# Embedding interaction tower: half of the bilinear units with the batch on the partitions, their sums over 64 on the free axis

## What is computed

```python
def _L0_rec_ref(emb_inputs, kernel):
    ...
    p = emb_inputs[:, ROW_IDX]
    q = emb_inputs[:, COL_IDX]
    return jnp.einsum('bne,hne,bnh->bn', p, kernel, q)
...
z = _L0_rec_ref(e, L0_rec_kernel)
h = jnp.concatenate([z, dense_ctx], axis=1)
h = jnp.maximum(h @ W_top1 + b_top1, 0.0)
h = jnp.maximum(h @ W_top2 + b_top2, 0.0)
y = h @ W_top3
```

## Time and profile before

| what | value |
|---|---|
| median of 3 runs | 486.28 us (486.17 to 489.33) |
| the profiled execution, its own time | 487.89 us |
| its span (first to last instruction) | 486.1 us |
| granted TensorE clock over the span | 0.995 of full |

### The profile page before, as it was taken

The page is one execution under the profiler, slowest core; times in us unless marked ns, Lnnn a source line. Parts: engine busy times, 40 slices in busy tenths (PEclk is TensorE's granted clock), DMA queues, the critical chain, the costliest instruction groups (busy, mean ns, idle before and its releaser), DMA issues.

```text
span 486.1 us, 8241 instructions
## 1 busy us (share of the span) xinstructions
PE 429.2 (88%) x3552; PEld 273.3 (56%) x3552; DVE 306.3 (63%) x321; ACT 35.3 (7%) x69; POOL 242.0 (50%) x260
## 2 busy tenths in 40 slices
PE   0225999999999999999999999999999999999976
PEld 0114665555566765555566766555566766555545
DVE  0114687777777367777776367777776367777730
ACT  1000000000011100000011100000011100000002
POOL 5777777777777777736077776506074000000000
PEclk9999899999999999999999999999999999999999
DMA  5787851111111111101011111001011000000000
GB/s 126 165 173 172 197 159 28 27 27 28 27 27 28 28 26 29 29 16 24 2 26 28 28 27 29 18 6 23 2 26 21 1 2 1 1 0 1 1 1 0
DMA packets 13620, 19.20 MB, mean 39 GB/s; under 512 B 5584, under 2 KB 6928, under 8 KB 13584
## 3 DMA queue, kind: packets, MB, share of 16 engines
q1 hardware_dynamic: 5392, 10.27, 9.1%
q0 software_dynamic: 8192, 8.40, 8.8%
HBM read 18.65 MB, written 0.00 MB: 38 GB/s over the span
## 4 chain that ended last, share of the span: by engine, by line
PE 69%; issue 12%; DVE 9%; POOL 6%; DMA 2%; ACT 1%; DVEq 0%
PE bil L390 35%; PE z_ps L412 24%; DVE prod L333 8%; POOL gathered L252 6%; PE side_ps L426 5%; PE side_ps L432 2%; PE bil L426 1%; DMA gathered<-in_tbl,ids_sb 1%; PE bil L359 1%; PE bil L432 1%; PE side_ps L438 1%; DMA ids_sb<-in_ids 0%; ACT emb L272 0%; DVE inner L329 0%; DVE inner L327 0%
## 5 line engine op out<-in xcount | busy, mean ns | idle before, releaser
L333 DVE TENSOR_TENSOR prod<-bil,emb 128x1024 f32<-128x1024 f32 x224 | 259.8, 1216 | 129.6 <-PE bil L390 127.6
L252 POOL DMA_INDIRECT gathered<-in_tbl,ids_sb x256 | 241.8, 944 | 129.3 <-issue 75.6
L390 PE MATMUL bil<-emb,k_sb 64*128 64x256 f32 x2048 | 257.4, 395 | 15.2 <-DVE prod L333 10.3
L390 PEld LDWEIGHTS bil<-emb,k_sb 64*128 64x128 f32 x2048 | 191.8, 191 | 79.3 <-DVE prod L333 32.7
L412 PE MATMUL z_ps<-prod,sel_sb 128*32 128x512 f32 x960 | 116.5, 595 | 2.3 <-DVE prod L333 2.3
L412 PEld LDWEIGHTS z_ps<-prod,sel_sb 128*32 128x32 f32 x960 | 30.0, 110 | 70.8 <-issue 59.7
L359 PE MATMUL bil<-ident_sb,gathered 64*128 64x64 f32 x256 | 15.2, 241 | 34.7 <-DMA gathered<-in_tbl,ids_sb 34.3
L272 ACT ACTIVATE emb<-bil 128x512 f32<-128x512 f32 x32 | 19.1, 596 | 287.7 <-PE bil L359 287.7
L325 DVE TENSOR_TENSOR prod<-bil,emb 128x512 f32<-128x512 f32 x32 | 21.8, 682 | 27.9 <-PE bil L390 27.9
L359 PEld LDWEIGHTS bil<-ident_sb,gathered 64*128 64x128 f32 x256 | 12.6, 147 | 44.8 <-issue 26.4
L412 PE MATMUL z_ps<-inner,sel_sb 128*32 128x512 f32 x64 | 29.1, 602 | 0.0
(11 more groups left out here) (17 smaller groups left out, 23.1 us busy)
## 6 DMA issues: line engine op xcount, KB each, us to landing
k_sb<-in_k_blocks SPq DMA_DIRECT2D x24, 256.0 KB, 5.1
gathered<-in_tbl,ids_sb POOLq DMA_INDIRECT x256, 2.5
k_sb<-in_k_blocks SPq DMA_DIRECT2D x8, 192.0 KB, 6.3
inner<-in_dense_rows SPq DMA_DIRECT2D x64, 1.0 KB
w_sb<-in_w SPq DMA_DIRECT2D x1, 1024.0 KB
k_sb<-in_k_blocks SPq DMA_DIRECT2D x8, 64.0 KB, 4.9
w_sb<-in_w SPq DMA_DIRECT2D x1, 512.0 KB
ids_sb<-in_ids SPq DMA_DIRECT2D x1, 128.0 KB, 2.2
```

The lines of the kernel that those rows point to most:

```text
L252: pool.indirect_dma_start(gathered[:, n % GATHER_RING, t, f * EMBED:(f + 1) * EMBED], None, tables[field], bass.IndirectOffsetOnAxis(ap=id ...
L333: dve.tensor_tensor(out, x_y[:, :, :], both.to_broadcast([P, 2, BANK]), ALU.mult)\
L390: last = pe.matmul(out[:, s, i * w:(i + 1) * w], k_sb[rows, n, :], e[rows, j, :], start=True, stop=True)
```

## The change

Of the 64 units of a chunk, 32 stay as they were (8 inner units and 24 "fields" units). The other 32 become "batch" units: the same work on 16 pairs of fields by 128 samples in place of 8 pairs by 256.

- `bilinear`: the weights are now the samples (`emb`, 64x128) and the moving operand four matrices side by side (`k_sb`, 64x512): two matmuls in place of four, the same columns in all. Samples come out on the partitions, 16 pairs x 64 numbers on the free axis.
- DVE multiplies 128x1024 by the gathered rows themselves (not the transposed ones) into a new ring `rows_prod` of four units (`ROWS_RING`).
- The sum over 64 is now on the free axis. For three of four batch units ACT makes it: 16 activations (copy) of 128x64 with an accumulator output, each writing its row back in place and one number into `z_rows`. For the fourth (`v % 4 == 3`) DVE makes it with one `tensor_reduce` of 128x1024.
- `reduce_batch` on PE is left only for the other 32 units, after every four of them (`BATCH_UNITS` = 4, `REDUCE_LAG` = 3 units later), into one bank for the whole chunk; `prod` has 6 slots.
- The dense layers get a fifth piece ahead, "turn": four 128x128 transposes of `z_rows`, which wait for all sums of the chunk, and one more copy on ACT in place of the second `copy_z`. The pieces now stand at units 6, 18, 25, 34 and 41 of the next chunk.
- All 32 fields of a chunk's gathered rows stay in SBUF for two chunks; from the third chunk on, POOL gathers when the chunk two before is multiplied. Quads are transposed four units ahead of their use, not three.

```diff
@@ -9,54 +9,112 @@
...
+BATCH_PAIRS = [0, 0, 2, 2, 2, 3, 3, 4]
 
 
 def unit_list():
-
-
     units = []
     for k in range(QUADS):
...
+        while batch or fields:
+            if len(batch) >= len(fields):
+                units.append(batch.pop(0))
+            else:
+                units.append(fields.pop(0))
     return units
...
+VECTOR_SUMS = {v for v in range(NB) if v % 4 == 3}
+NV, NA = len(VECTOR_SUMS), NB - len(VECTOR_SUMS)
+
+BIL_RING, PROD_RING, ROWS_RING, IN_RING = 3, 6, 4, 4
+BATCH_UNITS = 4
+BATCHES = NS // BATCH_UNITS
+REDUCE_LAG = 3
+SUM_LAG = 2
...
@@ -244,99 +312,145 @@
             pool.wait_ge(ids_loaded, 16)
             for n in range(NQUAD):
                 q, k = divmod(n, QUADS)
-                if n >= GATHER_RING:
-                    pool.wait_ge(quad_transposed, n - GATHER_RING + 1)
+                if q >= 2 and k == 0:
+                    pool.wait_ge(unit_multiplied, (q - 1) * NU)
...
+            def sum_rows(u):
+                q, (_, part, t) = u // NU, UNITS[u % NU]
+                v = batched_before(u)
+                if v % NB in VECTOR_SUMS:
+                    return
+                act.wait_ge(unit_multiplied, u + 1)
+                if q >= 2 and v % NB == 0:
+                    act.wait_ge(head_done, (q - 2) * len(PIECES) + 1)
+                col = 16 * FIRST_PARTS.index(part)
+                for x in range(16):
+                    row = rows_prod[:, v % ROWS_RING, x, :]
+                    last = act.activation(row, row, ACT.Copy, accum_out=z_rows[:, q % 2, t, col + x:col + x + 1])
+                last.then_inc(scalar_summed, 1)
...
+                if PIECES[i] == "turn":
+                    act.activation(z_sb[:, 2:4, :].rearrange("p g b -> p (g b)"), bank[:, 0:BANK], ACT.Copy).then_inc(head_kept, 1)
...
             for u in range(NUNIT):
                 for n in TRANSPOSED_AT[u]:
                     keep_quad(n)
+                if u >= SUM_LAG and UNITS[(u - SUM_LAG) % NU][0] == "batch":
+                    sum_rows(u - SUM_LAG)
...
+                if kind == "batch":
+                    v = batched_before(u)
+                    if v >= ROWS_RING:
+                        free_rows(v - ROWS_RING)
+                    row = gathered[:, q % 2, t, 2 * c * EMBED:(2 * c + 8) * EMBED].unsqueeze(1)
+                    dve.tensor_tensor(rows_prod[:, v % ROWS_RING, :, :].rearrange("p (j x) h -> p j (x h)", j=2),
+                                      x_y[:, :, :], row.to_broadcast([P, 2, BANK]), ALU.mult).then_inc(unit_multiplied, 1)
+                    return
...
+                dve.tensor_reduce(z_rows[:, q % 2, t, col:col + 16], rows_prod[:, v % ROWS_RING, :, :], AXIS.X, ALU.add)\
+                   .then_inc(vector_summed, 1)
...
+                if kind == "batch":
                     for s in range(2):
                         rows = slice(s * EMBED, (s + 1) * EMBED)
-                        if m is not None:
+                        last = pe.matmul(out[:, s, :], e[rows, m, t * P:(t + 1) * P],
+                                         k_sb[rows, 2 * part:2 * part + 4, :].rearrange("p n h -> p (n h)"),
+                                         start=True, stop=True)
+                    last.then_inc(unit_done, 1)
+                    return
...
+                if PIECES[i] == "turn":
+                    pe.wait_ge(scalar_summed, (q + 1) * NA)
+                    pe.wait_ge(vector_summed, (q + 1) * NV)
...
```

More of the change, by code:

```diff
@@ L15 @@
 HIDDEN1, HIDDEN2 = 512, 256
[L16 to L19, removed]
+CHUNK = 256
+CHUNKS = BATCH // CHUNK
+CT = CHUNK // P
 TILES = BATCH // P
@@ L25, with part_list @@
 BANK = 512
+GROUPS = 4
+def part_list():
+    parts = []
+    for k in range(QUADS):
+        parts.append((k, None, None))
+        for m in (2 * k, 2 * k + 1):
+            parts += [(k, m, 2 * cp) for cp in range(k)]
+    return parts
+PARTS = part_list()
+NPART = len(PARTS)
+BATCH_PAIRS = [0, 0, 2, 2, 2, 3, 3, 4]
 def unit_list():
@@ L32, in unit_list @@
     for k in range(QUADS):
-        units.append((k, None, None))
-        for m in (2 * k, 2 * k + 1):
-            units += [(k, m, 2 * cp) for cp in range(k)]
+        own = [n for n in range(NPART) if PARTS[n][0] == k]
+        units.append(("inner", own[0], 0))
+        couples = [(x, m) for x in range(0, k - 1, 2) for m in range(2)][:BATCH_PAIRS[k]]
+        firsts = [own[1 + m * k + x] for x, m in couples]
+        batch = [("batch", n, t) for n in firsts for t in range(CT)]
+        fields = [("fields", n, 0) for n in own[1:] if n not in firsts and n - 1 not in firsts]
+        while batch or fields:
[3 more added lines that the diff above has]
+                units.append(fields.pop(0))
     return units
@@ L76, in slot_row @@
 def slot_row(slot):
-    s = slot % 64
-    return slot // 64, 32 * (s % 4) + 2 * (s // 4)
+    return 32 * (slot % 4) + 2 * (slot // 4)
 def z_row(b, side):
[L83 to L87, removed]
+    s, n = divmod(b, 2 * NPART)
+    part, i = divmod(n, 2)
+    for first in (part, part - 1):
+        if first in FIRST_PARTS:
+            at = 16 * FIRST_PARTS.index(first) + 8 * s + 4 * (part - first) + 2 * i + side
+            return 2 + at // P, at % P
+    u = [v for v in range(NU) if UNITS[v][:2] in (("inner", part), ("fields", part))][0]
+    a = summed_before(u)
+    if UNITS[u][0] == "fields":
+        return i, slot_row(2 * a + s) + side
     if i == 1 and side != s:
[L89 to L93, removed]
+        return 0, slot_row(2 * a + 1) + side
+    return (s, slot_row(2 * a) + side) if i == 0 else (0, slot_row(2 * a) + s)
 FREE_ROWS = sorted({(g, r) for g in range(GROUPS) for r in range(P)}
@@ L101, in dense_of @@
 def dense_of(k, side):
-    bank, row = slot_row(2 * FIRST_OF[k] + 1)
-    return FREE_ROWS.index((2 * bank + 1, row + side))
+    return FREE_ROWS.index((1, slot_row(2 * summed_before(FIRST_OF[k]) + 1) + side))
 def pair_index(i, j):
@@ L185, in interaction_tower, with inner_batch @@
         block = ctx.enter_context(nc.Block())
[L187 to L193, removed]
+        def inner_batch(n):
             q, k = divmod(n, QUADS)
-            return q * NU + FIRST_OF[k]
+            return summed_before(q * NU + FIRST_OF[k]) // BATCH_UNITS
         @block.sync
@@ L261, in keep_quad @@
                 act.wait_ge(quad_transposed, n + 1)
-                if q >= 2:
+                if q >= 2 and k == 0:
                     act.wait_ge(unit_multiplied, (q - 1) * NU)
[L264 to L271, removed]
@@ L301, in _ @@
                     keep_head(*HEAD_AT[u], side_ps)
[L302 to L306, removed]
+            for u in range(NUNIT - SUM_LAG, NUNIT):
+                if UNITS[u % NU][0] == "batch":
+                    sum_rows(u)
+            keep_head(CHUNKS - 1, 0, side_ps)
+            copy_z(CHUNKS - 1)
+            for i in range(1, len(PIECES)):
                 keep_head(CHUNKS - 1, i, bil[i % BIL_RING][:, 0, :])
```

267 lines of the change are left out of this document (153 added, 114 removed).

## The result

The changed kernel takes 543.45 us (median of 4 runs, 542.18 to 543.92) against 487.8 for the kernel before (four runs, three of them those given ahead): a ratio of 1.1125, 95% interval 1.1052 to 1.1199. It is 11% slower. Its profiled execution took 542.18 us with a span of 540.4.

The account below looks back on a forecast made before the run. ScalarE was to bound the kernel at 101.8 us a chunk: first sum at 51, sums 378, other work 24, edges 48, end 19, around the span 1.8: 522 us profiled, 520 median; 8 in 10 range 450 to 640.

Parts of the forecast that it names:

- signs given: Middle chunks: ACT busy over 85%, DVE's idle time before L405 released by ACT, PE some 70%, a chunk near 118 us.
- What the change takes from PE and gives DVE: Per chunk: PE's reductions 14.3 us in place of 28.6, PE's sum 84.2; DVE gains 8 `tensor_reduce` of 1.1, sum 84.0.
- Rival (d): On PE, the 64x512 matmul takes 1.72 us, adding 27.5 us a chunk, 112 in all; about 520 us; chance 0.03.
- The step of ScalarE: One small activation with its accumulator readout on ACT takes 246 ns, the middle of 196 and 296; ends 124 and 396.
- that case: On ACT, activation and accumulator readout overlap at both ends: 124 + 72 = 196 ns a step.
- Rival (a): ACT's sums are cheap, 124 ns a step, holding up to about 180; PE and DVE bound; 456 us; chance 0.27.
- ScalarE becomes the bound: ACT's sum is 101.8 us a chunk, 18 more than PE's or DVE's.
- The failed step: A quad's copy on ACT stands behind up to three sums, 11.8 us; PE's wait for it was given nothing extra.
- The sum, term by term: Whole kernel: first sum at 51, 96 sums 378, ACT's other work 24, three edges 48; last sum ends at 501.
- The turn: At each chunk's edge ACT waits about 5 us for PE to make the transposes of `z_rows`.
- Handing over: In the kernel before, a chunk's 11 us over PE's sum of 98 are the handing over between PE and DVE.
- Rival (b): Three engines equally full at 196 ns a step, 22 us handing over, chunk 106, kernel about 480 us; chance 0.13.

## Why the prediction was right, and where it was off

The forecast was 522 us for the profiled execution and 520 for the median; measured 542.2 and 543.4. The direction held, and ScalarE's sums are what costs, but the size was short by 4%, and ScalarE's pace reaches PE by another way than forecast. Of the signs given, DVE's idle time before L405 was to be released by ACT: 14.1 us are, 71.9 by PE. PE's busy share fell to 78%, not 70, and a chunk takes 122.8, not 118.

*What the change takes from PE and gives DVE.* Right. `tensor_reduce` is 1206 ns long (1.1 taken for its pace), the products with the gathered rows 1215, the 64x512 matmuls run side by side: a unit takes 1.13 us beside DVE, as now. Rival (d) falls. DVE's sum was 84.0 and is 85.7 busy.

*The step of ScalarE.* 246 ns forecast, 239 measured, but by a way other than argued, and so by some luck. I had an activation of 224 ns, a readout of 172, and an overlap lost between them. They are 243 and 189 ns, and both boundaries overlap by 0.1 us: 145 + 94. By my own lengths that case was 196. The 243 ns agrees with the page of the Trainium skill that was weighed, "VectorE: DVE Perf Modes", section "The TRN2 errata — SBUF-src ops pay a fixed extra latency per instruction": by it an estimated 240 ns were to be expected for 64 elements from SBUF, and here the rows of PSUM sources misled by 19 ns. That page's difference between the two sources, an estimated 43 ns from its 52 cycles, is larger than these 19. The run without accumulator agrees with the other page of the Trainium skill, "ScalarE: Activation LUTs", section "What ACT_TABLE_LOAD costs": an estimated 146 ns a step by the page, 0.146 us measured. The PSUM rows agree with its lengths less well than the prediction says: 172 ns for two elements, where it gives an estimated 188. Rival (a)'s condition was false, but its time was right to 3%: with a step of 0.146 us the kernel takes 468, with next to none 463, against 456.

*ScalarE becomes the bound.* It is the fullest engine whose time is not stretched by the clock: 100.0 us a chunk, forecast 101.8. The run without accumulator shows that the sums' length is a cause: 75 us come and go with 93 ns a step. But "bound" was too strong. With the same sums on ScalarE and the copies elsewhere the kernel takes 497, so its busy share of 81% in a chunk (I wrote over 85%) was the sign of something else.

*The failed step* is the sentence "PE waits there too, but only while ACT is behind anyway, so I add nothing for it". The quads' copies behind sums are no free wait. They stop PE three times a chunk, the clock is at its lower level behind each of these waits, and DVE has nothing to multiply (it stands idle 5.22 us behind PE's wait of 5.29). ScalarE is idle 22.8 us in a chunk where I had 16 (5.4 for the piece `l2` of the dense layers, which stands behind PE's wait of 5.29, 4.8 for the turn, 4.1 for transposed quads, 2.8 for `copy_z`, the rest in small waits), and the run with the copies on DVE puts the price of their place at 9 us of idle time a chunk and their own work at 4. The sum, term by term: first sum at 52.3 (51); 96 sums 367 (378); other work 27 (24); idle time until the last sum, which ends at 519.1, 73 (48); from there to the end of the span 21.3 (19.0). The idle time is 25 us over, and the cheaper step hides 11 of them: that the total is only 20 us off is in part luck. At the end PE had waited 9.04 us for the last sums, and the last reduction took 3.59 us at the lower clock, where I had 1.8:

```profile
519.11 1.08 PE L535 MATMUL side_ps<-ident_sb,z_rows 128*128 128x128 f32 x4 [9.04 <-ACT rows_prod L349]
520.12 3.59 PE L524 MATMUL z_ps<-prod,sel_sb 128*32 128x512 f32 x16
```

*How much of that is the clock* stays open. PE's busy time in a chunk is 104.1 with the copies on ScalarE, 99.5 with them on DVE and 96.6 with almost no sums, so the stretches at half clock add some 5 to 8 us of busy time; no run kept the waits and took the clock away. Two things bound it. The sums placed later gave 25 us with the clock unchanged (0.907), so those came from the waits. And from the clock over the span (0.908 of 540 us) PE spent an estimated 99 us at the lower level, with the copies on DVE (0.948 of 495) 51 us; work at half speed loses at most half of such time, so of the 47 us between these runs an estimated 24 at most are lost to the clock directly.

*The turn* (about 5 us of waiting) was placed rightly, 4.82. Moved together with the other pieces it gave nothing back; what it costs alone no run shows. The longest stretch at the lower clock follows on ScalarE's late start behind it (294.8 to 305.1). With the pieces later only 3.4 us of it are left there, but others come elsewhere: the clock over the span is 0.903, where it was 0.908.

*Handing over.* The 11 us over the fullest engine's sum in the kernel before is no constant. It depends on how long PE leaves its units, as the batches of four show (3.9 us a chunk), and it was 18 in the two runs with half of the sums on DVE. Rival (b) could not be tried at its own step. Its 22 us of handing over are near what the run with three of eight sums on DVE shows: a chunk of 112.6, 23 over the 89.5 of DVE, the fullest engine whose busy time the clock doesn't stretch.

## What to carry to other kernels

A sum by activations with an accumulator is two instructions each: at 64 elements 0.239 us a step, of which 0.093 is the readout, so 16 of them cost 3.8 us where one `tensor_reduce` of the same 128x1024 costs 1.2. Before an engine with idle time gets work in long pieces, look at what short work it already has that another engine waits for: a 0.6 us copy behind three sums stopped TensorE for 5 us, and its clock was at the lower level for 5 us after that. And before moving work off the busiest engine, look at how it is cut up: halving the length of one kind of interruption, without moving anything, gave 4% here (quartering it, or one unit more of lag, only 1.5 to 1.8%), while the whole restructuring, with ScalarE free of charge, would have given 5%.

## What was not expected of the hardware

The readout of the accumulator shows as an instruction of its own, 189 ns long, that overlaps both its neighbours by 0.1 us, the activation whose sum it reads among them. An activation of 128x64 from SBUF takes 243 ns where the PSUM rows lead to 224. TensorE's granted clock was 1.2 GHz after single waits of 5.3 us, between long stretches at 2.4 GHz, and its longest stretch there, 10.2 us, began behind a wait of only 1.7 us, while the first unit behind a wait of 3.46 us still ran at 2.4 GHz.
